# A fused layer of gated delta attention and routed LoRA experts: router logits behind each transposition, a normalisation shared by two engines, and a recurrence loop of four chunks a pass

## The reference, cut to what matters

```python
xn = _layernorm(x, axis=-1)            # (x - m) / sqrt(var + 1e-5)
x = x + attention(xn) + ffn(xn)

def ffn(x):                            # 8 experts, 2 chosen per token
    scores = sigmoid(x @ W_router)     # the router logits
    _, topk_idx = top_k(scores + expert_bias, 2)
    ...                                # weights of the LoRA terms of gate, up and down
    return out

def attention(x):                      # 16 heads of 128
    q, k, v = silu(causal_conv4(x @ W.T)) for each; k *= DK ** -0.5
    a, beta = sigmoid(x @ Wa.T + ba), sigmoid(x @ Wb.T + bb)
    for t in range(512):               # per sequence and head, S is 128 x 128
        Sk = S @ k_t
        S = a_t[:, None] * S - (beta_t * (Sk - v_t))[:, None] * k_t[None, :]
        o_t = S @ q_t
    o = per_head_norm(o) * ln_g + ln_b
    return (o * sigmoid(x @ Wg.T)) @ Wo.T
```

## Time and profile before

| | us |
|---|---|
| median of 3 runs | 2592.14 |
| the profiled execution | 2592.64 |
| its span, first to last instruction | 2590.9 |
| PE busy in the span | 2181.5 (84%) |
| VectorE busy | 1925.3 (74%) |
| ScalarE busy | 1276.5 (49%) |
| stage 1 ends, FFN starts | 63.6 |
| first `head_sub` of the first chunk | 785.67 |
| first `head_sub` of the last chunk | 2165.87 |

### The profile page before, as it was taken

One profiled execution on the slowest core, in us unless ns is written; L12 is line 12 of the kernel. 1 busy time (PEld: TensorE's weight loads), 2 busy tenths in 40 slices (PEclk: granted clock), 3 DMA queues, 4 the chain that ended last, 5 costly groups with the idle time before them and its releaser, 6 DMA issues.

```text
span 2590.9 us, 61369 instructions
## 1 busy us (share of the span) xinstructions
PE 2181.5 (84%) x21482; PEld 1606.6 (62%) x21482; DVE 1925.3 (74%) x4379; ACT 1276.5 (49%) x2731; POOL 578.6 (22%) x577
## 2 busy tenths in 40 slices
PE   5999999999948777778878878777878786799998
PEld 3444888888836666667666667666666665344343
DVE  5222799999968889888888888988887898633334
ACT  2000677777833555445445455554544543334443
POOL 0000244444442222122222222221222222200000
PEclk9999999999977898898898898888888988899999
DMA  6000277777684555555555555555555556310210
GB/s 244 8 8 8 101 277 266 266 265 268 237 328 148 200 180 196 165 189 183 170 196 176 182 176 183 202 166 190 184 165 196 178 193 216 144 66 16 81 67 23
DMA packets 211170, 434.65 MB, mean 168 GB/s; under 512 B 47153, under 2 KB 160553, under 8 KB 181721
## 3 DMA queue, kind: packets, MB, share of 16 engines
q1 hardware_dynamic: 207880, 420.24, 46.9%
q10 hardware_dynamic: 2976, 10.72, 1.0%
q0 software_dynamic: 48, 0.16, 0.0%
HBM read 295.13 MB, written 136.98 MB: 167 GB/s over the span
## 4 chain that ended last, share of the span: by engine, by line
PE 51%; DVE 22%; issue 13%; ACT 11%; SPq 1%; DVEq 1%; DMA 1%; ACTq 0%; POOL 0%; POOLq 0%
PE PS L1379 10%; DVE arena L968 8%; ACT arena L769 4%; PE PS L1520 4%; PE PS L1275 4%; PE PS L1325 3%; PE PS L1252 3%; PE PS L1418 3%; PE PS L1354 3%; PE PS L1367 3%; PE PS L1406 3%; DVE arena L1059 2%; DVE arena L1002 2%; PE PS L1506 2%; PE PS L1393 2%
## 5 line engine op out<-in xcount | busy, mean ns | idle before, releaser
L1275 PE MATMUL PS<-arena 128*128 x2048 | 463.6, 386 | 1.8 <-DVEq L953 0.9
L968 DVE SCALAR_TENSOR_TENSOR arena<-PS,SM,arena 128x256 f32<-128x256 f32 x1152 | 452.8, 474 | 15.5 <-ACT arena L648 15.5
L1275 PEld LDWEIGHTS PS<-arena 128*128 128x128 f32 x2048 | 383.4, 188 | 82.1 <-DVE arena L968 6.5
L1379 PE MATMUL PS<-arena 128*128 128x128 f32 x1920 | 332.3, 326 | 76.5 <-ACT arena L774 75.3
L1379 PEld LDWEIGHTS PS<-arena 128*128 128x128 f32 x1920 | 281.3, 225 | 119.4 <-ACT arena L774 93.7
L575 POOL TENSOR_TENSOR arena<-arena 128x256 f32<-128x256 f32 x128 | 114.7, 896 | 1062.2 <-DVE arena L1074 1062.2
L769 ACT ACTIVATE arena<-arena 128x128 f32<-128x128 f32 x960 | 302.0, 395 | 0.0
L648 ACT ACTIVATE arena<-PS,SM 128x256 f32<-128x256 f32 x384 | 209.8, 565 | 88.9 <-PE PS L1275 84.1
L783 ACT COPY arena<-PS 128x256 f32<-128x256 f32 x240 | 89.6, 373 | 267.1 <-PE PS L1379 266.2
L795 ACT COPY arena<-PS 128x512 f32<-128x512 f32 (+1 forms) x188 | 91.0, 520 | 263.0 <-PE PS L1406 262.7
L1367 PE MATMUL PS<-ident,arena 128*128 128x128 f32 x960 | 177.4, 316 | 27.0 <-ACT arena L769 25.2
(11 more groups left out here) (135 smaller groups left out, 3549.5 us busy)
## 6 DMA issues: line engine op xcount, KB each, us to landing
arena<-g_d SPq DMA_DIRECT2D x126, 1024.0 KB, 5.1
arena<-vas_d SPq DMA_DIRECT2D x124, 384.0 KB, 3.3
vas_d<-arena SPq DMA_DIRECT2D x32, 1024.0 KB, 11.4
kq_d<-arena SPq DMA_DIRECT2D x8, 4096.0 KB, 11.5
arena<-kq_d SPq DMA_DIRECT2D x14, 2048.0 KB, 8.4
arena<-beta_d SPq DMA_DIRECT2D x8, 2048.0 KB, 9.1
kb_d<-arena SPq DMA_DIRECT2D x8, 2048.0 KB, 10.3
vas_d<-arena SPq DMA_DIRECT2D x8, 2048.0 KB, 12.4
```

The source lines that it names most:

```text
L968: nc.vector.scalar_tensor_tensor(acc, raw[:, :, i:i + PT_], CW[:, w, i, hh:hh + 1], acc, ALU.mult, ALU.add).then_inc(job_free if i == TAPS ...
L1275: ins = mm(dst.rearrange("p (b n) -> p b n", b=B), W4[:, w, kt, DH * h:DH * (h + 1)], XNT[:, kt, :, bass.ds(c * PT_ + (HALO - halo), halo ...
L1379: ins = mm(bank(7)[:, 128 * gi:128 * (gi + 1)].rearrange("v (l x) -> v l x", l=NB), STR[:, s % 2, gi, :], KQ[d][:, :, p0:p0 + 2].rearrange ...
```

## The change

It has four parts.

- **Norm.** ScalarE squares: four `ACTIVATE Square` for a group (one for each tile of 128 tokens), with the negated mean as bias, into two buffers in turn (`SG` and the joined `XAG`/`XAU`). VectorE keeps both sums and the reciprocal, and normalises from the input with one `tensor_scalar` for each tile (add, then multiply). Both engines are written with the groups staggered.
- **Router.** The logits of a group follow the transposition of the next group.
- **Transition.** Of the second chunk's `KB`, `KQ` and `EX` and of `VAS` 1 to 3, the loads move from ahead of the stores' end to behind the broadcast of L748, and so ahead of the `x_read` no-op.
- **Loop.** 3 passes of four chunks, then four chunks written out.

```diff
         def chunks(engine, chunk):
-            with engine.Fori(0, NS // 2 - 1) as i:
-                for c in range(2):
-                    chunk(i * 2 + c, i, c, True, True)
+            with engine.Fori(0, NS // 4 - 1) as i:
+                for q in range(4):
+                    chunk(i * 4 + q, i * 2 + q // 2, q % 2, True, True)
+            for c in range(2):
+                chunk(NS - 4 + c, NS // 2 - 2, c, True, True)
             chunk(NS - 2, NS // 2 - 1, 0, True, False)
             chunk(NS - 1, NS // 2 - 1, 1, False, False)
...
+            def squares(c):                                   # ScalarE
+                act.wait_ge(ln_mean, c + 1)
+                if c >= 2:
+                    act.wait_ge(ln_var, c - 1)
+                for n in range(4):
+                    ins = nc.scalar.activation(SQ[c % 2][:, n], XIN[:, 4 * c + n, :], ACT.Square, bias=ST8[:, 3, 4 * c + n:4 * c + n + 1])
+                ins.then_inc(ln_sq, 1)
...
+            squares(0)
+            squares(1)
+            deviation(0)
+            squares(2)
+            deviation(1)
+            transposed(0)
+            squares(3)
+            deviation(2)
+            transposed(1)
+            deviation(3)
+            transposed(2)
+            transposed(3)
+            act.wait_ge(logits, 4)
...
+            load_keys(0)                                      # ScalarE's queue
...
-            for m in range(4):
-                act.dma_start(VAS[:, m]...
+            load_values(0)
...
+            load_values(1)                                    # behind GB, ahead of x_read
+            load_keys(1)
+            for m in range(2, 4):
+                load_values(m)
             act.wait_ge(zeros, 5)
             nc.scalar.nop().then_inc(x_read, 1)
...
-                tt(XN[:, cs, :], XIN[:, cs, :], ST8[:, 3, cs].unsqueeze(2).to_broadcast([128, 4, D]), ALU.add).then_inc(ln_step, 1)
-                tt(SQ.rearrange("p (n d) -> p n d", n=4), XN[:, cs, :], XN[:, cs, :], ALU.mult).then_inc(ln_step, 1)
...
+                for n in range(4 * c, 4 * c + 4):             # VectorE, normalise(c)
+                    ins = nc.vector.tensor_scalar(XN[:, n, :], XIN[:, n, :], ST8[:, 3, n:n + 1], ST8[:, 4, n:n + 1], ALU.add, ALU.mult)
...
+            mean(0)
+            mean(1)
+            variance(0)
+            for c in range(4):
+                if c < 2:
+                    mean(c + 2)
+                normalise(c)
+                if c < 3:
+                    variance(c + 1)
...
+            transposes(0)                                     # TensorE
+            for c in range(1, 4):
+                transposes(c)
+                router(c - 1)
+            router(3)
```

More of the change, by code:

```diff
@@ L225, in build @@
         WT = take(NT)
-        XAG = take(CH)
-        XAU = take(CH)
+        XAf = take(2 * CH)
+        XAG, XAU = XAf[:, 0:CH], XAf[:, CH:2 * CH]
         SG = take(2 * CH).rearrange("p (s t) -> p s t", s=2)
-        SQ = SG.rearrange("p s t -> p (s t)")
+        SQ = [x.rearrange("p (n d) -> p n d", n=4) for x in (SG.rearrange("p s t -> p (s t)"), XAf)]
         HAD = take(CH)
@@ L597, in _, with deviation @@
             act.wait_ge(consts, 7)
-            for c in range(4):
+            def squares(c):
[5 more added lines that the diff above has]
+                ins.then_inc(ln_sq, 1)
+            def deviation(c):
                 act.wait_ge(ln_var, c + 1)
@@ L601, in _, with transposed @@
                                      bias=eps[:, 0:1], scale=1.0 / D).then_inc(ln_std, 1)
[L602 to L609, removed]
+            def transposed(c):
+                for k in range(2):
+                    act.wait_ge(xnT_psum, 2 * c + k + 1)
+                    nc.scalar.copy(XNT[:, k, c, HALO:HALO + T], bank(2 * c + k)).then_inc(xnT_ready, 1)
+            squares(0)
[11 more added lines that the diff above has]
+            act.wait_ge(logits, 4)
             nc.scalar.activation(SC[:, :, :], bank(0, 128).rearrange("p (n e) -> p n e", n=NX), ACT.Sigmoid).then_inc(scores, 1)
@@ L698, in _, with load_keys @@
             act.wait_ge(xnT_stored, 16)
-            for n in range(2):
+            def load_keys(n):
                 act.dma_start(KB[n].rearrange("k p t -> k (p t)"), kb_d[n:n + 1].rearrange("s k x -> k (s x)")).then_inc(kb_in[n], 16)
@@ L1205, in _, with transposes @@
             pe.wait_ge(consts, 9)
-            for c in range(4):
+            def transposes(c):
                 pe.wait_ge(xn_ready, c + 1)
@@ L1212, in _, with router @@
                     ins.then_inc(xnT_psum, 1)
-            pe.wait_ge(ld_small, 16)
-            pe.wait_ge(xnT_ready, 8)
-            for i in range(NX):
-                at = HALO + 128 * (i % 4)
-                for k in range(2):
-                    ins = mm(bank(0)[:, E * i:E * (i + 1)], XNT[:, k, i // 4, at:at + 128], WR[:, k, :], start=(k == 0), stop=(k == 1))
-            ins.then_inc(logits, 1)
+            def router(c):
+                pe.wait_ge(xnT_ready, 2 * c + 2)
+                for i in range(4 * c, 4 * c + 4):
+                    at = HALO + 128 * (i % 4)
+                    for k in range(2):
+                        ins = mm(bank(0)[:, E * i:E * (i + 1)], XNT[:, k, c, at:at + 128], WR[:, k, :], start=(k == 0), stop=(k == 1))
+                ins.then_inc(logits, 1)
+            pe.wait_ge(ld_small, 16)
+            transposes(0)
[3 more added lines that the diff above has]
+            router(3)
             for b in range(B):
```

29 lines of the change are left out of this document (16 added, 13 removed).

## The result

The changed kernel takes 2571.27 us (median; 2565.99 to 2578.29 over six runs, a seventh was disturbed and is left out). The kernel before, on the same chip, takes 2592.34 (2589.65 to 2593.99, 7 runs). The ratio is 0.9911, with a 95% interval of 0.9901 to 0.9921: 21 us faster by the medians, 23 by the ratio, 20 to 26 by its interval. The forecast was 2572. The profiled execution took 2571.75, its span is 2570.0. Note the spread already: before, the runs lie within 4.3 us, after within 12.3.

The account below looks back on a forecast made before the run. Five stages with different limits: serial VectorE then TensorE in stage 1, waiting for stores in the transition, branches mostly hidden in the recurrence. 12.2 + 7 + 1 = 20.2 us off 2592.1 gave 2571.9, predicted 2572, range 2566 to 2578.

Parts of the forecast that it names:

- Part 1: Norm and router: TensorE bounds from its second group on, logits end at 38.3 instead of 50.50 us; 12.2 us less.
- the square: ScalarE's square of 128x256 in the norm, not in the trace: 0.47 us taken half-way, 3.8 for eight.
- Rival 4: Router: TensorE's clock rises with transpositions between the logits, half of them at double speed, 3.5 us more, 2568; chance 0.06.
- The scaling: VectorE's scaling of 128x256 in the norm: 0.35 us each from a line between two widths, four overlapped 1.3 (0.7 to 2.2).
- Part 2: Transition: with loads moved from ahead of the stores, the first `head_sub` comes 7 us earlier (bounds 1 and 11).
- The gate: Transition: ScalarE's queue, with gather, broadcast and six moved loads, is late next; VectorE's addition waits for the no-op behind them.
- 20 to 24: Sign in the transition: GpSimd's clearing of the small tile comes 20 to 24 us earlier than 780.80.
- rival 1: Transition: the loads were not what held the stores, or ScalarE's queue is late; gains 1 us or less, 2578; chance 0.15.
- Part 3: Loop of the recurrence: four taken branches go, at 0.25 us each, 1 us in all (-1 to 5).
- mean of chunks 2 to 13 at 92.0 to 92.15: Sign in the recurrence: this mean chunk length in us; the forecast is wrong if it is off by more than 0.4.
- Rival 2: Loop: branches all on the path, four 4.2 us stalls in full 2556, at 1.27 each 2568; chance 0.08 (full 0.02).
- Rival 3: Recurrence: the clock pattern gets worse, 2612 with chunks at 0.78 (chance 0.02), or mildly 2579 at 0.85 (0.07).

Follow-up runs that it names:

- groups_behind: The kernel after with all four groups' transpositions first and the four groups of logits behind them; one run took 2576.17 us.
- router_between: The kernel before with only the changed router, a group's logits behind the next group's transposition; one run took 2584.71 us.
- the transition alone: The kernel before with only the deferred loads of the transition; 2584.84 us, ratio 0.9964.
- read_first: The kernel after with ScalarE's no-op, which VectorE's first addition waits for, moved ahead of the deferred loads; 2566.70 us, ratio 0.9894.
- loop4_alone: The kernel before with only the loop of four chunks a pass, 2 taken branches instead of 6; 2588.87 us, ratio 0.9982.
- after_loop2: The kernel after with the loop of two chunks a pass put back; 2571.43 us, ratio 0.9915.
- stage1_alone: The kernel before with only the norm and router of the change; 2579.60 us, ratio 0.9946.
- pad_eight: The kernel after with eight clearings of an unused tile on VectorE at the start of each chunk; 2580.49 us, ratio 0.9945.
- the unrolled kernel: The kernel after with the recurrence written out, no loop and no taken branch; 2573.92 us, ratio 0.9931.

## Why the prediction was right, step by step

**Part 1, -12.2 forecast, -13.84 measured.** The mechanism was as forecast: two table loads, the root, then TensorE as the bound. The logits end at 36.66 instead of 38.3. Of the 1.6 us 0.5 lie ahead of the second transposition (18.04, forecast 18.6): the square, taken at 0.47, took 3.30 / 8 = 0.41. The other 1.1 are TensorE's stretch, 36.66 - 18.04 = 18.6 instead of 19.7: logits start 1.76 us behind a transposition and the next transposition 3.27 behind them (19.80, 23.07), so that 5.03 us go for a group where I had added 1.97 and 3.45. Rival 4 did not come: a matmul of the logits lasts 0.214 us as before. The scaling (1.38 for four, forecast 1.3) was right. In `groups_behind` and `router_between` the logits ended within 0.3 us of the same working.

**Part 2, -7 forecast, -9.58 measured** in the kernel after, and 8.0 in the transition alone (7.8 with the loop of two). The gate was named rightly, as `read_first` showed by moving it: ScalarE's queue, not the stores. Off were the sizes. The sum itself gave 8, and I took 7 in case the stores were late, which they weren't: the clearing came 27.2 us earlier, where 20 to 24 was the sign. The gather's issue began 1.0 us later than forecast (751.93 + 13.84 against 764.8). The gather was issued in 3.38 us, not 4.89, and had landed 1.75 us behind it (757.06 less 755.31), where I took 3.5 without a row; the six deferred issues took 3.9, not 3.0. The stores gained 13.4 us (753.57 + 13.84 against 780.80), more than the 10.7 of freed DMA time, so rival 1 is refuted: q1 has 57.8% where it had 7.6%. Why it was more than the freed time was not tried; two executions differ by 1.8 us there.

**Part 3, -1 forecast.** Against the measured 2.4 us the wrong way it looks like a miss in the sign, but nothing shows that the branch did it. The kernel with the loop of two has the same time within what its runs can tell. What moved is chunk 0 (+4.8), chunk 1 (+1.4) and, the other way, chunk 8 (-2.9 against 92.15). The long chunk 0 is not repeated: of the nine other profiles with the deferred loads eight have a chunk 0 of 90.8 to 91.6 us, and one 93.05. The step of the prediction, that what a branch costs in one chunk is given back in the next, is supported by the pairs and by the equal sums with two, six and no branches; its words "mean of chunks 2 to 13 at 92.0 to 92.15" were missed by 0.15 (91.85), because it had no term for a single short chunk. Rival 2 is refuted in its full form, 17 us. At 1.27 us a branch it is refuted by the profiles, whose sums are equal, but not by the times: `loop4_alone` gained 4.7 us (2 to 7) where four branches went, the kernel after nothing clear over `after_loop2`. What the loop is worth by itself, between nothing and 5 us, is open. Rival 3 did not come: the mean chunk was no longer, and only chunks 0 and 1 were at 0.82 and 0.83.

**The sum.** The stages were underestimated by 1.6 and 2.6 us, and the recurrence by 3.4 the other way. That the total came within 1 us of 2572 is in part luck, since these errors cancel and the runs of this one kernel lie 12 us apart. By the ratios, stage 1 and the transition alone make 0.0054 x 2593.6 = 14.0 and 0.0036 x 2593.6 = 9.3, in all 23.3, and both together without the loop of four 0.0085 x 2593.6 = 22.0: these two add up. The loop's 4.7 on top would make 28, and the kernel after has 0.0089 x 2592.34 = 23.1, so the loop's part does not add up with the others.

**What stays open.** What starts a chunk that is 3 us short or long. In the profiles a long one among the twelve has the clock at 0.82 and a short one at 0.90. Both orders occur: in `stage1_alone` the low clock came without a delay ahead of it, in `pad_eight` the delay came first. What sets the places where the clock falls in the one and not in the other was not found. Nor was it tried whether work added inside the serial part of a chunk, and not in VectorE's wait, is swallowed; only the unrolled kernel speaks for it, whose VectorE was busy for 0.66 us more a chunk than that of `read_first`.

## What to carry to other kernels

Price each edit in its own stage by the wait that ends last there, and check afterwards whether the shift arrives where the next long stage starts, and again where it ends: here 13.8 and 8 to 9.6 us arrived whole at the recurrence, which in one profiled execution (`stage1_alone`) gave 5.1 of them back. In a long loop whose period is the same with and without a stall, count a saving inside the period at nothing until the mean period moves; and where work must be deferred, put the signal that others wait for ahead of the deferred issues, which brought the recurrence's start 3.3 us forward here. Before adding work to test a theory, read whether the engine is waiting at that very place.

## What the runs showed of the hardware

- Twelve chunks of the recurrence take 1105.8 to 1106.1 us in one execution each of eight kernels, with none, two or six taken branches and VectorE busy for 948 to 960 us of them. In five others they take 3 to 4 us more or less, by one chunk.
- The same stretch of a chunk, the sixth, takes 10.30 us at a granted clock of 0.85 to 0.89 and 13.00 us at 0.50 (`stage1_alone`, and chunk 8 of the kernel after).
- A taken branch stalls VectorE too: its first addition of a pass comes after 3.01 us of idling in the kernel after, where it is hidden in the wait for `carried`, and at the exit from the loop it comes at once. With eight clearings the idling is 4.00 us.
- Two queues with packets of unlike size: q1's share of the DMA engines went from 7.6% to 57.8% in the 16 us that answer to each other, when the loads beside it moved 2.99 MB instead of 6.19.
- Straight-line code went with more work on VectorE here: the unrolled kernel's twelve chunks have it busy for 959.58 us, against 951.72 in `read_first`, whose twelve chunks are as long (1105.92 and 1106.11). Of the difference 6.7 us lie in the additions on 128x64, 384 of them in both; why wasn't tried.
